# Graph attention with its group norm inside, in a periodic order

## What is computed

```python
# group norm over (time, node, channels of a group), 32 groups, eps 1e-5, per batch
def _gat(h, adj, Wq, Wk, Wv, Wo, bo):          # h: (128 graphs, 128 nodes, 128)
    q = (h @ Wq).reshape(BT, N, HEADS, HD)     # k and v likewise, 4 heads of 32
    scores = jnp.einsum('bnhd,bmhd->bhnm', q, k) / math.sqrt(HD)
    scores = jnp.where(adj[None, None] == 0, -1000000000.0, scores)
    attn = jax.nn.softmax(scores, axis=-1)
    o = jnp.einsum('bhnm,bmhd->bnhd', attn, v).reshape(BT, N, D_MODEL)
    return h + o @ Wo + bo
```

## Time and profile before

| What | us |
|---|---|
| Median of three runs (lowest to highest) | 4762.72 (4756.2 to 4768.53) |
| The profiled execution | 4768.75 |
| Its span in the profile | 4767.0 |
| Busy over the span: PE, DVE, ACT, POOL | 3674.7, 3217.7, 2612.5, 2507.2 |
| Group norm, to the end of its last DVE operation | 103.55 |
| Attention, first transpose to the end of POOL's last operation | 113.28 to 698.9 |

### The profile page before, as it was taken

One profiled execution on the slowest core, in us unless ns is written; L12 is line 12 of the kernel. 1 busy time (PEld: TensorE's weight loads), 2 busy tenths in 40 slices (PEclk: granted clock), 3 DMA queues, 4 the chain that ended last, 5 costly groups with the idle time before them and its releaser, 6 DMA issues. The chain is left out here.

```text
span 4767.0 us, 82846 instructions
## 1 busy us (share of the span) xinstructions
PE 3674.7 (77%) x29132; PEld 2400.7 (50%) x29164; DVE 3217.7 (67%) x6212; ACT 2612.5 (55%) x5079; POOL 2507.2 (53%) x2873
## 2 busy tenths in 40 slices
PE   5767655999999999999999968653886596648757
PEld 2555542555555555555555536521665463336636
DVE  3565552888888888888888834261897675229864
ACT  1444434777777777777777611001566555318553
POOL 2444546778787788877777520000676532002560
PEclk8888875999999999999999986576776887769778
DMA  2000010000000000000000022024121224470133
GB/s 75 12 14 16 14 27 17 4 19 19 19 19 19 19 18 15 15 19 19 19 19 17 21 75 72 2 87 165 59 79 42 63 64 115 164 227 23 47 96 102
DMA packets 363569, 231.29 MB, mean 49 GB/s; under 512 B 44096, under 2 KB 334344, under 8 KB 361096
## 3 DMA queue, kind: packets, MB, share of 16 engines
q1 hardware_dynamic: 363160, 225.98, 16.5%
HBM read 150.15 MB, written 75.76 MB: 47 GB/s over the span
## 5 line engine op out<-in xcount | busy, mean ns | idle before, releaser
L1100 DVE TENSOR_TENSOR_SCAN mam_hs<-mam_dA,mam_ps_b 128x1024 f32<-128x1024 f32 x512 | 1156.1, 2274 | 2.2 <-PE mam_ps_b L905 2.1
L919 PEld LDWEIGHTS mam_ps_h<-mam_ident,mam_hs 128*128 128x128 f32 x4096 | 460.6, 146 | 420.9 <-issue 417.4
L1038 ACT ACTIVATE mam_dA<-mam_dt,mam_A 128x496 f32<-128x496 f32 x1024 | 649.4, 703 | 0.7
L905 PE MATMUL mam_ps_b<-mam_DB,mam_dtxt 32*128 32x512 f32 x2048 | 583.1, 645 | 85.1 <-DVE mam_hs L1100 81.6
L919 PE MATMUL mam_ps_h<-mam_ident,mam_hs 128*128 128x128 f32 x4096 | 585.0, 288 | 27.5 <-ACT mam_hTb L1046 26.3
L1046 ACT COPY mam_hTb<-mam_ps_h 128x512 f32<-128x512 f32 x768 | 424.8, 583 | 317.4 <-PE mam_ps_h L919 313.4
L703 POOL TENSOR_SCALAR mam_tap<-mam_xcp,mam_cw 128x512 f32<-128x512 f32 x192 | 301.1, 1568 | 18.7
L1110 DVE COPY mam_hTb<-mam_ps_h 128x512 f32<-128x512 f32 x256 | 175.7, 686 | 173.1 <-PE mam_ps_h L919 173.1
L261 POOL TENSOR_TENSOR gat_ex<-gat_ex,gat_den 128x512 f32<-128x512 f32 x128 | 133.1, 1041 | 292.2 <-DVE gat_den L482 292.1
L931 PE MATMUL mam_ps_y<-mam_hTb,mam_WC 128*32 128x128 f32 x8192 | 279.9, 277 | 0.4 <-issue 0.4
L931 PEld LDWEIGHTS mam_ps_y<-mam_hTb,mam_WC 128*32 128x32 f32 x8192 | 211.3, 110 | 124.2 <-issue 94.9
(11 more groups left out here) (663 smaller groups left out, 8675.9 us busy)
## 6 DMA issues: line engine op xcount, KB each, us to landing
moe_wg<-in_L_ffn_weight SPq DMA_DIRECT2D x32, 1024.0 KB, 7.7
rnn_xr<-x SPq DMA_DIRECT2D x23, 512.0 KB, 5.8
l1y_wh<-mode_weights SPq DMA_DIRECT2D x16, 544.0 KB, 3.7
h<-gat_out SPq DMA_DIRECT2D x32, 256.0 KB, 2.3
mam_ht<-h SPq DMA_DIRECT2D x128, 64.0 KB, 2.0
mam_hr<-h SPq DMA_DIRECT2D x128, 64.0 KB, 2.0
mam_xt<-in_x SPq DMA_DIRECT2D x128, 64.0 KB, 2.0
x<-mam_out SPq DMA_DIRECT2D x128, 64.0 KB, 1.8
```

The source lines that it names most:

```text
L905: last = pe.matmul(ps_b[w % 2][:, n, :], steps[r, g * P:(g + 1) * P], DB[r, g, :, :].rearrange("p s t -> p (s t)"), start=True, stop=True, ...
L919: last = pe.transpose(ps_h[n][:, q * P:(q + 1) * P], hs[:, w % 3, c:c + P], ident[:, :])
L1038: act.activation(dA[:, h, :, n, 1:], dt[:, i % 2, h, :].rearrange("p (q t) -> p q t", q=Q)[:, :, 1:], ACT.Exp, scale=A[:, h, n:n + 1]).the ...
L1100: dve.tensor_tensor_scan(hs[:, w % 3, :], dA[:, h, first:first + 2, :, :].rearrange("p q s t -> p (q s t)"), ps_b[w % 2][:, :, :].rearrang ...
```

## The change

The call of `group_norm` before attention goes; `graph_attention` reads `x` itself (`group_norm` stays for a later layer).

* **Load and sums.** `x` comes in 16 chunks of eight rows straight into `hg`. ACT squares each chunk into a ring of three. PE sums with a matrix of ones of only 32 columns; the four halves (two of the rows, two of the squares) go to the four column tiles of one bank (`tile_position=(0, 32 * q)`). The eight weights are loaded after the fourth chunk.
* **Factors.** Per batch DVE reduces the bank to 128x32, a small matmul with `sel` brings mean and mean square to 32 partitions (one per group), POOL takes the root of 32x1, and two matmuls spread scale and offset: per channel down the partitions (`colsc`) and along the row (`rowsc`, with `bo` in it).
* **Application.** The raw rows are turned; ACT's copy into `hT` becomes an activation with `colsc` as scale and bias. The residual is normalized by POOL: `normed_times` multiplies, `normed_plus` adds (in place of `bias`).
* **Copies.** All four `pT` copies are ACT's.
* **Order.** Each step of a group has a place; steps of consecutive groups are 64 places apart, and each queue runs its steps by place plus 64 times the group. Semaphores of the head steps exist once per head. `z` has three buffers instead of two. The mask constant `BIG` is 2^100 instead of 1e30.

```diff
-def graph_attention(nc, hg, adj, Wq, Wk, Wv, Wo, bo, gain, shift, h0, tag="gat", eps=1e-5):
+def graph_attention(nc, x, adj, Wq, Wk, Wv, Wo, bo, gain, shift, h0, tag="gat", eps=1e-5):
...
+        def due(w, place):
+            i, left = divmod(w - place, STEPS)
+            return i if left == 0 and 0 <= i < N else None
...
+            for j in range(NC):
+                b, t0 = divmod(j * CH, T)
+                sp.dma_start(hg[:, j * CH:(j + 1) * CH, :], x[b, t0:t0 + CH].rearrange("t w c -> w t c")
+                             ).then_inc(xin[j], 16)
...
+            def normed_times(i):
+                pool.wait_ge(turned, i + 1)
+                times[i] = step.mark(pool.tensor_tensor(
+                    hg[:, group(i), :], hg[:, group(i), :],
+                    rowsc[:, batch_of(i), 0, :].unsqueeze(1).broadcast_to(wide), ALU.mult))
...
+            def groups(b):
+                pe.wait_ge(red_ready, b + 1)
+                pe.matmul(ps_p[0][0:G, 4 * b:4 * b + 4], red[:, b, :], sel[:, :], start=True, stop=True
+                          ).then_inc(grouped, 1)
...
+                pe.wait_ge(squared, j + 1)
+                v, v2 = chunk(j), sq[:, j % 3, :]
+                for q, src in enumerate((v[:, 0:512], v[:, 512:1024], v2[:, 0:512], v2[:, 512:1024])):
+                    last = pe.matmul(ps_s[b][32 * q:32 * q + 32, :], ones[:, :], src, start=(j % PER == 0),
+                                     stop=(j % PER == PER - 1), tile_position=(0, 32 * q))
+                last.then_inc(sums_done, 1)
+                if b and j % PER == 0:
+                    groups(b - 1)
+                if b and j % PER == 2:
+                    channels(b - 1)
...
+            pe.wait_ge(norm_ready, B)
...
-                act.copy(hT[:, i % 2, :], ps_f[:, :]).then_inc(hT_ready, 1)
+                act.activation(hT[:, i % 2, :], ps_f[:, :], ACT.Identity, scale=colsc[:, b, 0:1], bias=colsc[:, b, 1:2]
+                               ).then_inc(hT_ready, 1)
...
-            def probs_in(i, h):
-                dve.wait_ge(flipped, i * H + h + 1)
...
-    with nc.sbuf_tensor("hg0", [P, BT, C], f32) as hg:
-        group_norm(nc, d["x"], hg, "gn0")
-        graph_attention(nc, hg, *layer("L0_conv", "adj", "Wq", "Wk", "Wv", "Wo", "bo", "ns_g", "ns_b"), h0)
+    graph_attention(nc, d["x"], *layer("L0_conv", "adj", "Wq", "Wk", "Wv", "Wo", "bo", "ns_g", "ns_b"), h0)
```

More of the change, by code:

```diff
@@ new lines, in graph_attention @@
+                "out_ready", "dch", "pch"))
+        squared, sums_done, red_ready, grouped, gv_ready, gs_ready, wide_ready, spread, norm_ready = (
+            s.sem(n) for n in ("squared", "sums_done", "red_ready", "grouped", "gv_ready", "gs_ready", "wide_ready",
+                               "spread", "norm_ready"))
+        scored = [s.sem(f"scored{j}") for j in range(2)]
+        peaked, exped, summed, p_ready, flipped, pT_ready = (
+            [s.sem(f"{n}{h}") for h in range(H)] for n in ("peaked", "exped", "summed", "p_ready", "flipped", "pT_ready"))
@@ L222, in graph_attention @@
         stored = [s.sem(f"stored{j}") for j in range(3)]
+        xin = [s.sem(f"xin{j}") for j in range(NC)]
         LOADS = 8
+        SLOTS = range(0, (N + 7) * STEPS)
+        rows = h0.rearrange("(i r) w c -> i w r c", r=R)
         block = ctx.enter_context(nc.Block())
-        STEPS = range(-1, N + 3)
-        rows = h0.rearrange("(i r) w c -> i w r c", r=R)
-        def turn(i):
-            return 0 <= i < N
+        def due(w, place):
+            i, left = divmod(w - place, STEPS)
+            return i if left == 0 and 0 <= i < N else None
@@ L280, in finish @@
                 pool.tensor_tensor(o, o, shift_b[:, :].unsqueeze(1).broadcast_to(wide), ALU.add).then_inc(out_ready, 1)
-            for i in STEPS:
-                if turn(i - 3):
-                    finish(i - 3)
-                if turn(i):
-                    divide(i, 0)
-                if turn(i - 2):
-                    deviations(i - 2)
-                if turn(i):
-                    divide(i, 1)
-                    divide(i, 2)
-                if turn(i + 1):
-                    bias(i + 1)
-                if turn(i):
-                    divide(i, 3)
+            for w in SLOTS:
+                i = due(w, 66)
+                if i is not None:
+                    normed_times(i)
+                for h, place in ((0, 139), (1, 132), (2, 184), (3, 143)):
+                    i = due(w, place)
+                    if i is not None:
+                        divide(i, h)
+                i = due(w, 133)
+                if i is not None:
+                    normed_plus(i)
+                i = due(w, 276)
+                if i is not None:
+                    deviations(i)
+                i = due(w, 393)
+                if i is not None:
+                    finish(i)
@@ new lines, in _ @@
+            pe.wait_ge(made, 1)
+            for j in range(NC):
+                b = j // PER
+                pe.wait_ge(xin[j], 16)
+                pe.wait_ge(squared, j + 1)
[8 more added lines that the diff above has]
+                    channels(b - 1)
@@ L323, in scores @@
                                          start=False, stop=(r == R - 1), tile_position=(h * D, 0))
-                last.then_inc(scored, 1)
+                last.then_inc(scored[pair], 1)
             def project_q(i):
```

315 lines of the change are left out of this document (195 added, 120 removed).

## The result

| What | before | after |
|---|---|---|
| Median of the runs, us | 4762.72 | 4501.91 (4496.7 to 4502.82) |
| The profiled execution, us | 4768.75 | 4496.7 |
| Its span, us | 4767.0 | 4495.0 |
| First transpose, us | 113.28 | 44.70 |
| Interval between groups, mean of the 31, us | 17.24 | 10.79 |

The ratio of the times is 0.945, its 95% interval 0.9427 to 0.9472. The forecast was 4498, the time is 4502.

What follows compares the result with a forecast made beforehand. Order, not work, bound attention: engines waiting round a ring three groups deep. Attention ends at 42 + 52 + 296 + 41 = 431 us; 698.9 - 431 - 3 saves 265, giving 4504, or 4498 on the median's footing; range 4462 to 4552.

Steps and rivals of the forecast that it cites:

- Start, 42 us: Program head, loads and norm: first transpose at 42 us instead of 113.3, bounds 39 and 46.
- First five intervals, 52 us: Start of attention: POOL has no `finish` or root yet, so PE's 10.4 us per interval holds, 52 us.
- PE's sum, 10.44 us: Attention, per group: PE's matmuls back to back at full clock take 10.44 us.
- Steady interval, 11.4 us: Attention, the other 26 intervals: 11.4 us each with DVE and POOL blocking each other, bounds 10.44 and 12.4.
- POOL loses 4 x 0.26: Attention: if all four `scale` meet a POOL operation, POOL loses 1.0 us per interval and needs 11.1.
- The rival built on it: Attention: DVE and POOL block fully at every `scale`; interval 12.4 us, 26 us more, 4524; chance 0.20.
- Activation with scale and bias: Attention, ACT: the activation into `hT` was priced equal to the copy it replaces.
- PE as the bound (10.44): Attention: `scale` falls into POOL's pauses, interval 10.44 us, 25 us less, 4473; chance 0.17.
- A gap on PE: Attention: one long PE wait lowers the clock; interval about 12.9 us, 39 us more, 4537; chance 0.08.
- Half clock through attention: Attention: PE stays at half clock, 20.9 us per interval, slower than before at 4798; chance 0.04.
- The signs of being wrong: Attention: granted clock below 1.00, any single wait per interval over 2 us, or ACT's activation dearer than a copy.
- The end, 41 us and 8.4: After the last transpose: 41 us of POOL work, then 5.4 us plus 3 for more semaphores until mamba's load.

Runs made afterwards that it cites:

- the kernel with the extra matmuls: The changed kernel plus four PE matmuls whose result nobody reads, around the last batch's sums and before the first transposes; median 4489.9 us.
- the order with the plain copy: The changed kernel with the old group norm in front as its own stage, `hT` a plain copy and POOL only adding the bias; median 4564.3 us.
- the kernel with `mix` back: The changed kernel with `mix` on PE moved from place 210 to 187, right behind the flips of heads 3 and 2; median 4538.0 us.
- The sums one by one: The changed kernel with all four column-sum matmuls of a chunk in one column tile, one behind the other; median 4523.5 us.

## Why the prediction held, point by point

**Start, 42 us: held, 44.70.** The chunks land 2.5 us later than worked out, at 36.5 (a stretch from 12 to 16 us, where the weights are loaded, moved only 206 GB/s; why, no run asked). The tiles overlap as priced. The chain took 8.15 us from the last square on instead of 7.5; its small DVE operations are 0.14 to 0.16 instead of 0.2, the root 0.54 (taken as 0.6), but two matmuls ran at a half clock that I had not foreseen.

**First five intervals, 52 us: held by two errors.** They took 11.12 + 8.32 + 9.28 + 10.24 + 10.24 = 49.2. Without flips, scores of the second pair and `mix` of earlier groups an interval is shorter than PE's full sum, which I overlooked: at full clock the five take 45.8 (the kernel with the extra matmuls). The half clock until 55 us gives about half of that back. In the second profile of the same kernel it lasts until 78 us and costs some 9.6 us more. That my forecast held to 0.1% has luck in it.

**PE's sum, 10.44 us: it is 10.24.** That was the interval wherever PE was the full engine.

**Steady interval, 11.4 us: right mechanism, wrong size and, in part, wrong reasoning; it is 11.04.** I had said that by a collision each makes the other wait, and took a value near POOL's 11.1. The runs show DVE as the full engine and POOL next to unslowed: its divides take 1.05 us on average, where one of before took 1.04, and the one divide per interval that starts while a free `scale` operation runs takes 1.07. So the step that failed is "POOL loses 4 x 0.26"; it loses some 0.02 us, and waits 0.42 us for the end of `scale` before `finish`. The row that I had it from the earlier trace rows shows POOL stretched, but mostly beside two DVE operations of another kind, each with two tensors as sources:

```profile
1239.19 0.88 DVE L1135 SCALAR_TENSOR_TENSOR mam_po<-mam_po,mam_e 128x512 f32<-128x512 f32 x1
1240.11 0.77 DVE L1136 SCALAR_TENSOR_TENSOR mam_po<-mam_po,mam_e 128x512 f32<-128x512 f32 x1
```

Of the 512 operations of POOL's line 733 in the kernel before, the 93 that run beside one of these two lines take 0.58 to 0.85 us, and all others but one take 0.39 to 0.42. That one took 0.56, beside two `tensor_scalar` of 128x128 as in `scale`, so an operation of that kind can hold POOL up by some 0.16 us; in attention it rarely did.

On DVE's side I had priced the full lock at 5.0 us for four operations; they take 2.80, because two of the four still pass at 0.34. On the other hand `ve` was missed: a 128x4 operation, by its work not worth a line, costs 0.6 us more. Put right, DVE's sum is 12.4 - 2.2 + 0.6 = 10.8; with the 0.25 us per interval in which DVE stands (0.27 of 12 in the stretch shown) that is the 11.04. My 11.4 came near it as a value taken between POOL's 11.1 and DVE's 12.4, for a reason that does not hold; that is luck. The page "SBUF — State Buffer" of the Trainium skill (section "Who interferes with whom"), by which the later of the two blocks fully for the whole operation, describes DVE's side of the rows: waits until POOL's operation has ended. For POOL's side they show no more than the 0.02 us above, and the one case of 0.16; what a longer DVE operation of this kind does to POOL, no run shows. The rival built on it failed only in the count of operations that meet one.

**Activation with scale and bias: wrong, without effect.** It takes 0.78 us instead of the copy's 0.59. ACT is not full, and the order with the plain copy has no shorter interval (11.07).

**Rivals.** PE as the bound (10.44) was not the case but lies just below: taking the collision away gives it. A gap on PE costs its own length, as the kernel with `mix` back shows, but the clock's part of that rival did not come at a gap of 1.0 us. The sums one by one cost 26.8 us where 23 were named. Half clock through attention did not happen; it happened at its start, at a price of 5 to 15 us.

**The signs of being wrong.** Of the three that I had named, two came up. The granted clock in attention was below 1.00, at its start only (0.52 from 44 to 56 us), and the activation is dearer than a copy. A single wait of over 2 us did not occur in the steady intervals, though ACT's for `gat_neg` comes close (48.1 us in 25 waits, 1.9 each); the 2.6 in that row lies behind the last transposes. What I had expected to see differs in detail as well: PE is busy 97% and not 92, the four `scale` operations take 2.80 us and not 3 to 5, and POOL's are not stretched.

**The end, 41 us and 8.4: held.** From the last transposes (379.63) to POOL's last end (421.56) it is 41.9, and 7.9 to mamba's load.

**The sum.** Saved up to mamba's first load: 274.9 us, 9.9 more than forecast, of which 2.9 are lost in the rest of the program; 272.0 in the profile against 265 forecast. The median fell by 260.8, since the profiled run of before lay 6.0 above its median and that of after 5.2 below. So the agreement of the medians to 4 us is closer than that of the parts.

## What to carry to other kernels

Lay the interval out for the fullest engine first, with no matmul waiting for a copy that is made just before it (a deeper pipeline by itself was not tested), and then look for the operation whose single durations spread: its median against its minimum shows a block that the busy share hides. A DVE operation that runs beside a busy POOL can be worth more in a shape that is slower alone. And where PE stands in a short serial chain, cheap matmuls that nobody reads can keep its clock for the work behind.

## What the runs showed of the hardware

* A blocked DVE `tensor_scalar` lasts until the POOL operation beside it has ended, and in attention POOL was hardly slowed: `scale` 0.333 us alone and up to 1.314, POOL's divide 1.05 on average and 1.07 where it starts while a free `scale` operation runs.
* DVE's `scalar_tensor_tensor` with two tensors as sources does stretch POOL's operations: 0.58 to 0.85 us in 93 cases, 0.39 to 0.42 without it (one of 0.56, beside two `tensor_scalar`).
* Size is no protection: a `tensor_scalar` of 128x4 took 0.170 us free and 0.775 blocked. `tensor_reduce` (0.67 to 0.69) and `reciprocal` (0.18) of the same engine kept their times beside a busy POOL.
* The same operation with a destination of 3 x 43 against a source of 129 was never blocked: 0.377 to 0.406 us in 128 cases, with POOL busy 97% of a steady stretch.
* Four column tiles, 128x512 each in f32: four passes in 0.45 us, against 1.72 one behind the other.
* In all nine profiles with this start and without the extra matmuls TensorE's clock fell to 0.50 at the same point (idle 0.87, 2.03 and 0.80 us around three tiny matmuls). It came back some 11 us after the first transposes in four of them and some 33 us after in five. What decides between the two is open; with the extra matmuls it did not fall, in either profile.
